# An audio tower on one core: spectra in parts of 384 and 256 columns, tangent and fold on VectorE, first magnitude products ahead of the angle, and more filler transposes

## The reference

```python
xp = x.reshape(B, C, S, 200)                       # x: (8, 64, 1000), so 5 patches for each channel
fr = jnp.fft.rfft(xp, axis=-1)                     # 101 frequencies
feats = concatenate([abs(fr), angle(fr)], -1)
h = gelu(feats @ W1 + b1) @ W2 + b2                # 202 -> 808 -> 128, 2560 rows
...
h = h + attn(layernorm(h))                         # state space model: tanh scan with 32 states over
                                                   # 320 steps; A_bar from an inverse of a 32 x 32 matrix
...
h = h + ffn(layernorm(h))                          # gated recurrence, hidden 256, 320 steps
```

## Time and profile before

| | |
|---|---|
| median of 3 runs | 895.92 us (894.9 to 898.41) |
| profiled execution | 894.79 us, span 893.0 us |
| PE, PEld | 829.9 us (93%), 700.3 us (78%) |
| DVE, ACT, POOL | 578.6 us (65%), 369.8 us (41%), 89.7 us (10%) |
| mean granted TensorE clock | 0.581 |
| chain that ended last | PE 85%, ACT 6%, DVE 4%, issue 3%, DMA 1% |

### The profile page before, as it was taken

How to read it: one execution, slowest core, us unless ns; L and a number is a source line. 1 busy time by engine, 2 the same in 40 slices (tenths; PEclk the granted TensorE clock), 3 DMA queues, 4 the chain that set the end, 5 groups by cost and what they waited for, 6 DMA issues and landing times.

```text
span 893.0 us, 40450 instructions
## 1 busy us (share of the span) xinstructions
PE 829.9 (93%) x17013; PEld 700.3 (78%) x17013; DVE 578.6 (65%) x3480; ACT 369.8 (41%) x2016; POOL 89.7 (10%) x205
## 2 busy tenths in 40 slices
PE   7889999989999999999999999999999998988875
PEld 5667666778888888888888888888888887877765
DVE  5243527376676776767767777677667777676654
ACT  5465766433343433433434334334333343343222
POOL 4212204110000000100000001000000000000000
PEclk6699999955555555555555555555555555555555
DMA  7100000000000000000000000000000000000000
GB/s 173 35 1 1 1 1 1 1 3 3 7 3 7 6 4 6 7 3 7 4 6 7 3 7 6 4 6 3 7 6 4 6 7 3 6 4 5 6 3 8
DMA packets 7452, 8.51 MB, mean 10 GB/s; under 512 B 1343, under 2 KB 6557, under 8 KB 7271
## 3 DMA queue, kind: packets, MB, share of 16 engines
q1 hardware_dynamic: 6965, 5.92, 2.8%
q0 software_dynamic: 256, 0.01, 0.0%
q10 hardware_dynamic: 50, 0.00, 0.0%
HBM read 4.62 MB, written 1.31 MB: 7 GB/s over the span
## 4 chain that ended last, share of the span: by engine, by line
PE 85%; ACT 6%; DVE 4%; issue 3%; DMA 1%; POOL 0%; POOLq 0%
PE ps L1511 42%; PE ps L1517 11%; PE ps L1313 8%; PE ps L1372 5%; PE ps L1423 3%; PE ps L1387 3%; PE ps L1525 3%; DVE h_hi L478 2%; PE ps L1431 2%; ACT addend L866 2%; PE ps L1295 1%; PE ps L1302 1%; PE ps L1283 1%; PE ps L1231 1%; PE ps L1247 1%
## 5 line engine op out<-in xcount | busy, mean ns | idle before, releaser
L1511 PE MATMUL ps<-h_hi,w_first 128*128 128x8 f16 x2552 | 267.3, 170 | 28.4 <-DVE h_hi L478 28.0
L1511 PEld LDWEIGHTS ps<-h_hi,w_first 128*128 128x128 f16 x2552 | 219.9, 104 | 90.9 <-DVE h_hi L478 90.9
L1511 PE MATMUL ps<-h_hi,w_rest 128*128 128x8 f16 x5104 | 276.3, 168 | 0.0
L1511 PEld LDWEIGHTS ps<-h_hi,w_rest 128*128 128x128 bf16 x5104 | 240.6, 105 | 0.1
L856 ACT ACTIVATE tanh_r<-ps 128x16 f32<-128x16 f32 x320 | 58.6, 183 | 252.3 <-PE ps L1517 251.7
L1517 PE MATMUL ps<-h_lo,w_first 128*128 128x8 f16 x2560 | 160.0, 168 | 0.1
L1511 PE MATMUL ps<-rh_hi,w_first 128*128 128x8 f16 x1276 | 136.6, 173 | 12.1 <-DVE rh_hi L1133 1.0
L1511 PEld LDWEIGHTS ps<-rh_hi,w_first 128*128 128x128 f16 x1276 | 109.6, 104 | 39.0 <-DVE rh_hi L1133 1.3
L1511 PE MATMUL ps<-rh_hi,w_rest 128*128 128x8 f16 x2552 | 138.6, 168 | 0.0
L478 DVE TENSOR_TENSOR_SCAN h_hi<-coef,addend 128x32 f16<-128x32 f32 x320 | 73.1, 228 | 85.7 <-ACT addend L866 85.7
L1511 PEld LDWEIGHTS ps<-rh_hi,w_rest 128*128 128x128 bf16 x2552 | 121.8, 105 | 0.0
(11 more groups left out here) (211 smaller groups left out, 1421.6 us busy)
## 6 DMA issues: line engine op xcount, KB each, us to landing
x_sb<-in_x SPq DMA_DIRECT2D x4, 500.0 KB
out<-res SPq DMA_DIRECT2D x20, 64.0 KB, 2.0
W_sb<-in_L_tok_W SPq DMA_DIRECT2D x1, 606.0 KB
W_sb<-in_L_tok_W SPq DMA_DIRECT2D x1, 384.0 KB
wnat<-in_L_ffn_Wwr SPq DMA_DIRECT2D x1, 256.0 KB, 5.4
wnat<-in_L_ffn_Wwz SPq DMA_DIRECT2D x1, 256.0 KB, 11.2
wnat<-in_L_ffn_Ww SPq DMA_DIRECT2D x1, 256.0 KB, 10.5
wunat<-in_L_ffn_Wur SPq DMA_DIRECT2D x1, 128.0 KB, 6.9
```

Source lines behind the costliest of these rows:

```text
L1511: mm(gate(c, j, g, m), w[:, m * 128:(m + 1) * 128], state[:, k * NB:(k + 1) * NB], start=False, stop=False, skip_group_check=True)
```

## The change

- The two parts of a spectrum are cut at 384 (`HS`) as the groups are, not at 320, and the angle is counted done part by part: a group waits for its own.
- `tangent` and `fold` go from GpSimd to VectorE. The fold is now one instruction, 2 x arctangent minus PI or 0, so W1 is no longer doubled.
- `WARM` is 52, and further transposes of the identity (`busy`, 6 or 12 at a time) stand between the first steps of TensorE.
- `up(0, 0, 0)` and `up(0, 1, 0)` stand ahead of the wait for the angle.
- In group 0 the spectra of part 1 and what hangs on them are one piece earlier (`SPECTRA_LATE` = 1). Blocked Newton slots: (0, 6, 1), (2, 5, 1) and (4, 5, 1) in, (1, 0, 0) and (1, 1, 0) out.
- The five transposes of recurrence weights stand at pieces 0, 1, 4, 5, 6 of group 5 in place of 1 to 5.

```diff
-WARM = 26
+WARM = 52
+BUSY = 6
...
-WEIGHTS_AT = {(5, 1): 0, (5, 2): 1, (5, 3): 2, (5, 4): 3, (5, 5): 4}
+WEIGHTS_AT = {(5, 0): 0, (5, 1): 1, (5, 4): 2, (5, 5): 3, (5, 6): 4}
...
-SPECTRA_LATE = 2
+SPECTRA_LATE = 1
...
+    HS = 0, GM, PT
...
-            return t[:, h * HT:(h + 1) * HT]
+            return t[:, HS[h]:HS[h + 1]]
...
-            if (n, m, slot) in ((1, 0, 0), (1, 1, 0)):
+            if (n, m, slot) in ((0, SQRT_PIECE + 2, 1), (2, SQRT_PIECE + 1, 1), (4, SQRT_PIECE + 1, 1)):
...
+            def tangent(g, h):
+                x = half_of(absim[:, g, :], h)
+                dve.wait_ge(rden_done, 2 * g + h + 1)
+                dve.wait_ge(absim_done, 2 * g + h + 1)
+                v.tensor_tensor(x, x, half_of(rdenom, h), ALU.mult).then_inc(tang_done, 1)
+
+            def angle(g, h):
+                dve.wait_ge(atan_done, 2 * g + h + 1)
+                v.scalar_tensor_tensor(out=half_of(neghalf[:, g, :], h), in0=half_of(absim[:, g, :], h), scalar=2.0,
+                                       in1=half_of(neghalf[:, g, :], h), op0=ALU.mult,
+                                       op1=ALU.subtract).then_inc(fold_done, 1)
...
             add_power(0, 0)
-            read_spectra(0, 1)
+            read_im(0, 1)
             denominator(0, 0)
+            read_re(0, 1)
             add_power(0, 1)
             invert(0, 0)
             denominator(0, 1)
+            tangent(0, 0)
             invert(0, 1)
+            tangent(0, 1)
             sign(0)
-            dve.wait_ge(w1_in, 32)
-            v.tensor_scalar(W1_sb[:, 1, :], W1_sb[:, 1, :], 2.0, None, ALU.mult).then_inc(su_dve, 1)
-            angle(0)
+            angle(0, 0)
+            copy_patches(1, 0)
+            angle(0, 1)
+            copy_patches(1, 1)
...
                 if n % 2 == 1 and g < NP:
                     invert(g, 1)
+                    tangent(g, 1)
...
                     invert(g, 0)
+                    tangent(g, 0)
...
+            def busy(count, b):
+                for _ in range(count):
+                    tr(bank(b)[:, 0:128], ident[:], ident[:])
...
+            busy(BUSY, 7)
+            pe.wait_ge(w1_in, 32)
+            pe.wait_ge(mag_done, 1)
+            pe.wait_ge(su_act, 3)
+            for m in range(2):
+                up(0, m, 0)
             pe.wait_ge(su_act, 6)
...
-                if n % 2 == 0:
-                    pe.wait_ge(ang_done, n // 2 + 1)
+                pe.wait_ge(ang_done, n + 1)
                 for m in range(MC):
-                    up(n, m, 0)
+                    if n or m > 1:
+                        up(n, m, 0)
```

More of the change, by code:

```diff
@@ L619, in body @@
                         tok_head(LATE_ROWS[CH * c + j][0])
-            tangent(0)
-            fold(0)
-            pool.wait_ge(ang_done, 1)
+            pool.wait_ge(ang_done, 2)
             even_odd(pool, pool, 2)
@@ L732, in _ @@
             act.wait_ge(bias_psum, 1)
-            a.activation(biasT[:], bank(4)[:, 0:32], ACT.Copy).then_inc(su_act, 1)
+            a.activation(biasT[:], bank(6)[:, 0:32], ACT.Copy).then_inc(su_act, 1)
             for i in range(6, EARLY):
@@ L1230, in spectra, with up @@
                 for dst, table, part in ((ps_re(g, h), cos_sb, evenT), (ps_im(g, h), sin_sb, oddT)):
-                    last = mm(dst, table[:], part[:, h * HT:(h + 1) * HT], start=True, stop=True)
+                    last = mm(dst, table[:], part[:, HS[h]:HS[h + 1]], start=True, stop=True)
                 last.then_inc(spec_psum, 1)
+            def up(n, m, half):
+                t0, nq = group(n)
+                p = MC * n + m
+                k = msize(m)
+                feats = (magT, angT)[half]
+                last = mm(ps_hid[p % 2][0:k, 0:nq * CT], W1_sb[:, half, m * 128:m * 128 + k],
+                          feats[:, t0:t0 + nq * CT], start=half == 0, stop=half == 1)
+                if half == 1:
+                    last.then_inc(hid_psum, 1)
             def wait_newton(i):
@@ L1247, in newton @@
                     mm(ps_nx, DY[:], DY[:, 0:2 * N], start=True, stop=True).then_inc(nx_psum, 1)
+            def busy(count, b):
+                for _ in range(count):
+                    tr(bank(b)[:, 0:128], ident[:], ident[:])
             pe.wait_ge(consts, 1)
-            for _ in range(WARM):
-                tr(bank(6)[:, 0:128], ident[:], ident[:])
+            busy(WARM, 6)
             transposes(0, 0)
             transposes(0, 1)
+            busy(BUSY, 6)
             pe.wait_ge(su_dve, 2)
@@ L1261, in _ @@
             spectra(0, 1)
+            busy(2 * BUSY, 0)
             pe.wait_ge(su_dve, 11)
@@ L1365, in serial @@
                     ssm_step(k // CH, k % CH, k == 0)
-            def up(n, m, half):
-                t0, nq = group(n)
-                p = MC * n + m
-                k = msize(m)
-                feats = (magT, angT)[half]
-                last = mm(ps_hid[p % 2][0:k, 0:nq * CT], W1_sb[:, half, m * 128:m * 128 + k],
-                          feats[:, t0:t0 + nq * CT], start=half == 0, stop=half == 1)
-                if half == 1:
-                    last.then_inc(hid_psum, 1)
             def down(n, m):
```

78 lines of the change are left out of this document (33 added, 45 removed).

## The result

The changed kernel takes 891.58 us (median of 20 runs, 889.93 to 892.66), the kernel before in the same rounds 895.96 us (20 runs, 892.12 to 898.63): ratio 0.9956, 95% interval 0.9943 to 0.9969. That is 4.4 us less, where 9.3 us were forecast. The time lies in the range given, 0.2 us above the 891.4 under which the prediction would have called it faster, and the likeliest case did not come about as described.

The account below looks back on a forecast made before the run. Ahead of an unchanged recurrence of some 715 us, TensorE bounds the kernel, with a few waits and a lower clock. Terms -4.8 - 0.8 - 2.0 - 0.5 - 1.2 = -9.3 us, from the median 895.92 to 886.6 us; range 881.5 to 892.5.

Parts of the forecast that it names:

- the likeliest case: The whole forecast: all gains before the recurrence come, sum -9.3 us, time 886.6 us; chance 0.52.
- term B: Start of group 1: spectra one piece earlier shorten the wait for VectorE's row read, part moving to Newton 28; -0.8 us.
- C: Group 1: with the shorter wait the clock likely stays up, so the stretch runs at full speed; -2.0 us.
- rival 4: A new wait on VectorE or ScalarE eats the gains behind the start, clock up; 891.5 us, chance 0.12.
- Term A: Start, to group 0's second down product: earlier angle and products at full clock, if it stays up; -4.8 us.
- Rivals 1 to 3: At the start: clock dips at 15-25 us (0.22); stays low to about 39 us (0.08); fillers only load TensorE (0.06).
- Tangent on VectorE, parts of 384 and 256: At the start, ahead of the first angle: both tangents there 1.0 us earlier.
- Magnitude products first: Group 0: two magnitude products run ahead of the first angle product, 0.70 us each at the full clock.
- Group 2's slot: Group 2: the blocked Newton slot removes a wait of 0.50 us for a Newton copy; -0.5 us (0 to -0.8).
- Term D: Group 5: weight-copy wait goes (-1.7 us), BbarT later (+0.9, of that 0.44 hidden), no new wait; together -1.2 us.

Follow-up runs that it names:

- e2: The changed kernel with 12 filler transposes ahead of the Newton half step that waits in group 1: 885.42 us, ratio to before 0.992.
- e1: The changed kernel with the blocked Newton slots of before: 884.85 us, ratio to before 0.9903.
- e12: The changed kernel again, unedited, in the rounds of e9 to e11: 891.92 us, ratio to before 0.996.
- e3: The changed kernel with 26 warm-up transposes and no other fillers: 894.64 us, ratio to before 1.0006.
- e11: The kernel before with only the warm-up of 52 transposes and the fillers added: 891.76 us, ratio to before 0.9964.
- e5: e1 with the warm-up of 52 transposes but no later filler: 891.16 us, ratio to before 0.9952.
- e8: e1 with the tangents back on GpSimd, the split at 384 and the fold on VectorE kept: 885.86 us, ratio to before 0.9899.
- e7: e1 with both first magnitude products of group 0 behind the angle's wait again: 884.18 us, ratio to before 0.9897.
- e10: e9 with both magnitude products of group 0 behind the angle's wait (e7's edit): 886.47 us, ratio to before 0.9903.
- e4: The changed kernel with the recurrence weights' transposes at pieces 1 to 5 of group 5, as before: 891.52 us, ratio to before 0.9991.
- e6: e1 with group 0's spectra of part 1 one piece later, as before the change: 890.76 us, ratio to before 0.9952.
- e9: e1 with blocked slots (1,0,0) and (2,5,1), (1,1,0) free, and fillers in waits of groups 1 and 3: 887.2 us, ratio to before 0.9921.

## Why the forecast was half right

- **The step that failed** stands under term B: "1.5 us of it moves ahead, to Newton 28. But it is shorter than 2.49, and the clock is then likely to stay up." Place and size of the wait were right (1.48 us). But I took the length of a wait as the measure, with one wait of 1.70 us that left the clock up and waits of 2.46 and 2.49 in which or behind which it fell as my only rows. Behind this shorter one the clock fell, for twice as long as before. B and C were forecast at -2.8 us and came out at +3.3 (the lead from 4.63 to 1.29). With the wait filled and the clock up through the whole of group 1 (e2) they came out at -1.4 (lead from 4.11 to 5.50). So 4.7 us of the miss are the clock, and 1.4 would have been missing without it: the changed slots set TensorE back by 1.4 us against those of before (e1, whose -2.8 is the forecast's number with another order of slots). No rival had this case: rival 4 had the new wait, but with the clock up, and that its 891.5 us is nearly the measured time is luck.
- **Term A** was right, -4.8 forecast and -4.63 measured (-4.25 in e12), and its reason too: patch transposes 0.9 us late (0.2 forecast), first angle product at 29.47 (29.3), second down product at 37.27 (37.1). e3 and e11 show from both sides that the clock makes it. Rivals 1 to 3 are out. The working added the changed kernel's steps at full speed, and that held. That the number came out so close is in part luck: the clock rose at 6.2, not near 5, which put the patch transposes 0.7 us behind the forecast, and from there to Newton 6 (26.28, 26.1 forecast) the working was 0.5 us too long. Between 20 and 25 us TensorE was busy 4.86 of 5 us.
- **The Trainium skill's rule** ("TensorE: Matmul & The Clock Gate", Part 4: PE-mode transpose), by which the fillers would be pure load, does not hold for these fp32 transposes: the clock rose between 4.5 and 7.7 us in all thirteen kernels' traces, while TensorE had done nothing but fp32 transposes of the identity, and without fillers behind the warm-up the second down product of group 0 came 5.1 us (e3) and 6.0 us (e5) later.
- **Tangent on VectorE, parts of 384 and 256:** both tangents 0.8 us earlier (1.0 forecast). The engine gives 0.2 of it (e8); the rest is probably the shorter second part, which no run took by itself. With the clock low at the start none of it shows at the second down product (e3).
- **Magnitude products first:** in the working they cost their 1.4 us in the chain and gave it back later. They take 0.5 us net (e7, e10).
- **Group 2's slot:** -0.5 forecast, -0.49 measured (1.41 to 1.90 of lead).
- **Term D:** -1.2 forecast, -1.2 measured (1.90 to 3.09), but not by its parts. BbarT's wait is again 0.43, not 0.8 to 1.3: without the weight transposed ahead of it, it is 0.86 (e4), so reciprocal and tangent made BbarT late by 0.4 and not by 0.9. They do take their time, but the four AbarT instructions behind them, 1.09 us before beside GpSimd's tangent, now take 0.48. And a wait of 0.55 us for the Gelu at 147.95 is new, where I had said that none would be. The two errors nearly cancel.
- **Chances:** 0.8 on faster by over 0.5% was too much for a gain that hung on one unproved sentence about the clock. A fall behind the new wait should have been a rival of its own: with C gone, the sum is -7.3 us, and with a longer fall less.

## What to carry to other kernels

When a change moves a wait, ask what the clock does behind the new place, and price both answers; a shorter wait was no safer here. Idle time at a known place that can't be removed is better cut in two (e1: 5.7 us by the recurrence's start, for one line) or filled with transposes that depend on nothing (e2). Test a bundle by its parts: the fillers alone gave what the whole bundle gave (e11), and the choice of blocked slots, one line, took back what the rest would have added (e1).

## What the runs showed of the hardware

- The length of the one wait does not decide whether TensorE's clock falls. After 1.48 us it fell each time, 0.9 to 3.0 us later (changed kernel, e12, e3, e4), behind 1.70 us (before, e4, e11) it did not; behind 1.13 us in group 3 it fell in e2 and in no other kernel that has this wait, the changed kernel with the same work around it among them.
- Once low at these places, it stayed low for 13.65 us (changed kernel, e12), 10.24 (e3 at this place, e4, e6, e11), 6.8 (before) and 3.4 (e2), with TensorE at work throughout (in e11 after 0.4 us). Why the same seam gives different lengths stays open.
- The recurrence, the same instructions in all kernels, took between 706.1 and 709.3 us from step 0 to step 319. The changed kernel alone took 706.19 in one execution and 708.35 in the other (e12), the kernel before 708.02. An edit ahead of it that is worth less than that is better read at the recurrence's start than in the total.
- The moment at which the clock first rises differs between executions (4.5 to 7.7 us), and with it the end of the 52 transposes: the patch transposes began at 8.90 in e9 and at 9.97 in e12. Their start lies between 8.87 (e11) and 10.29 (e6) in the kernels with 52, as much as several of the edits are worth. In e1 it is 9.50 with a rise at 4.91: there VectorE could start on the input at 8.11 only, in e9 and the changed kernel at 7.51.
- VectorE is slower while GpSimd works. The fold of 384 columns takes 0.55 to 0.56 us three times in the changed kernel with GpSimd idle, and 1.50 at 147.01, with GpSimd working for 1.44 of it; the four AbarT instructions take 0.48 (changed kernel, e1, e4) against 1.09 (before) and 1.22 (e8) beside GpSimd's tangent. So a move of work from GpSimd to VectorE can cost less than its own time.
